# A mixture-of-experts stage rebuilt: plain scatters in place of adding ones, up weights fetched by address on VectorE

## What is computed

```python
h = tok(x)                                      # gather 36 angles per token, 6-qubit circuit, 192 features
h = h + attention(layernorm(h))                 # one head of 192, 512 x 512 scores per batch
z = layernorm(h)
scores = z @ Wg                                 # 8 experts
top2, which = top_k(scores, 2); share = softmax(top2)
h = h + sum_k share[k] * (gelu(z @ W1[which[k]] + b1[which[k]]) @ W2[which[k]] + b2[which[k]])
```

## Time and profile before

| What | us |
|---|---|
| median of 3 runs | 336.73 |
| lowest and highest of them | 336.37, 339.21 |
| span of the profiled execution | 338.6 |
| TensorE busy, matmuls | 240.9 |
| VectorE busy | 177.6 |
| ScalarE busy | 95.2 |
| POOL busy | 250.2 |

### The profile page before, as it was taken

One profiled execution on the slowest core, in us unless ns is written; L12 is line 12 of the kernel. 1 busy time (PEld: TensorE's weight loads), 2 busy tenths in 40 slices (PEclk: granted clock), 3 DMA queues, 4 the chain that ended last, 5 costly groups with the idle time before them and its releaser, 6 DMA issues. The chain is left out here.

```text
span 338.6 us, 6221 instructions
## 1 busy us (share of the span) xinstructions
PE 240.9 (71%) x1585; PEld 162.0 (48%) x1585; DVE 177.6 (52%) x698; ACT 95.2 (28%) x223; POOL 250.2 (74%) x283
## 2 busy tenths in 40 slices
PE   0831973668478989768654899999999587999500
PEld 0621641223243445444421678777777365877400
DVE  5758997488998866684699322232222122122200
ACT  1002001354324144634233323332432132133000
POOL 5778979309968777766777388888883888888673
PEclk9999995558955556965555599999999799699955
DMA  6710019900000001111123146656461556564510
GB/s 191 201 13 11 0 45 400 382 5 2 2 0 9 12 13 60 63 57 60 59 70 103 22 54 69 64 62 67 53 69 18 60 62 65 61 69 50 59 10 0
DMA packets 28141, 22.61 MB, mean 67 GB/s; under 512 B 15434, under 2 KB 25546, under 8 KB 27787
## 3 DMA queue, kind: packets, MB, share of 16 engines
q0 software_dynamic: 13296, 7.95, 21.1%
q1 hardware_dynamic: 14524, 14.23, 13.0%
q10 hardware_dynamic: 288, 0.03, 0.1%
HBM read 7.25 MB, written 15.63 MB: 68 GB/s over the span
## 5 line engine op out<-in xcount | busy, mean ns | idle before, releaser
L709 POOL DMA_INDIRECT out<-up x71 | 110.3, 1554 | 33.1 <-issue 13.9
L1972 PE MATMUL bank_b<-down,up 128*128 x426 | 91.2, 354 | 5.0 <-DVE up L1473 1.0
L1972 PEld LDWEIGHTS bank_b<-down,up 128*128 128x128 f32 x426 | 72.9, 200 | 22.6 <-issue 18.8
L1473 DVE TENSOR_SCALAR up<-bank_b,up 128x192 f32<-128x192 f32 x71 | 29.6, 418 | 97.5 <-PE bank_b L1972 84.9
L657 POOL DMA_INDIRECT routed<-rows,slot x64 | 61.9, 968 | 23.9 <-issue 18.0
L472 POOL DMA_INDIRECT theta_all<-angles,ids x32 | 32.4, 1012 | 10.9 <-issue 9.0
L1651 ACT ACTIVATE up<-bank_a 128x384 f32<-128x384 f32 x71 | 31.3, 497 | 3.4 <-PE bank_a L1962 2.9
L1775 PE MATMUL bank_b<-queries_t,keys_t 32*128 32x512 f32 x64 | 26.1, 900 | 6.9 <-ACT keys_t L1499 3.4
L1782 PE MATMUL bank_a<-keys_t,wt 32*128 32x512 f32 x64 | 27.6, 949 | 3.8 <-DVE nmax L1133 2.1
L1663 ACT COPY up<-bank_c 128x384 f32<-128x384 f32 x18 | 8.6, 478 | 61.8 <-PE bank_c L1951 58.7
L1133 DVE TENSOR_REDUCE nmax<-bank_a 128x2 f32<-128x1024 f32 x16 | 19.5, 1219 | 11.5 <-PE bank_a L1782 11.3
(11 more groups left out here) (420 smaller groups left out, 369.4 us busy)
## 6 DMA issues: line engine op xcount, KB each, us to landing
routed<-pad_rows SPq DMA_DIRECT2D x8, 528.0 KB, 5.7
out<-hres SPq DMA_DIRECT2D x8, 384.0 KB, 2.4
down<-down_w SPq DMA_DIRECT2D x1, 2304.0 KB, 11.9
up<-up_w SPq DMA_DIRECT2D x1, 1536.0 KB
out<-up POOLq DMA_INDIRECT x71, 3.5
up<-routed SPq DMA_DIRECT2D x69, 16.0 KB
routed<-rows,slot POOLq DMA_INDIRECT x64
up<-up_w SPq DMA_DIRECT2D x1, 780.0 KB
```

The costliest lines, as they stand in the source:

```text
L709: pool.indirect_dma_start(out=out_rows, out_offset=bass.IndirectOffsetOnAxis(xb[:, m // STEP % RING, m % STEP, DEST:DEST + 1].bitcast(I32) ...
L1473: dve.tensor_scalar(y[:, m % RESULTS, :], bank_b[:, m % 2, 0:D], xb[:, m // STEP % RING, m % STEP, SHARE:SHARE + 1], None, ALU.mult).then_ ...
L1972: mm = pe.matmul(bank_b[:, m % 2, 0:D], hid[:, m % STEP, c * P:(c + 1) * P], down[:, bass.ds(first + c * D, D)], start=(c == 0), stop=(c = ...
```

## The change

The experts' results are no longer added into `out`. They are scattered as plain rows into a tensor of their own, read back and added to `hres` on VectorE, and `out` is written once.

- **Scatters.** POOL's indirect DMA of a result writes to `shares_out`, 8192 rows of 192: row `k * 4096 + token` for choice k. `DEST` carries that number. No two blocks write one row, so the waits for blocks with common tokens, the table behind them and SyncE's counting go. POOL waits for the landing of block m - 4 (LAG) before it issues block m, and tells of it by `landed`.
- **Runs.** The blocks are put in another order: first the whole blocks that the first four batches fill, by expert, then those that each later batch completes, then the rest. The number of blocks stays 71. So results of early batches are complete before the last block. Of the blocks, 24 (EARLY) can be loaded before the second half's scatters have landed.
- **Table.** `block_table` holds a block's numbers in the partition of the block's own number, two per partition, so it works on 48 or so elements at a time where it had up to 568. Thirteen dependent stages follow its first.
- **Loads.** All 71 blocks have their own place in `xb` (no ring), and SyncE issues all loads, each behind its own value load.
- **Up weights.** TensorE merges each expert's up weights into 128 partitions, with the same 16 rows eight times over, and ScalarE copies them beside the down weights, into `wide` (eight copies). In the expert stage `pick_up`, `expert_of` and ScalarE's copy go. VectorE's `expert_up` reads the expert's address (`value_load`) and copies 32 partitions x 384 into `up_now`, four times a step.
- **Sums.** SyncE reads the two choices of a batch back (`load_sums`, 786 KB), VectorE adds them to `hres` (`add_experts`, four additions), and SyncE stores the batch. For batches 0 to 5 that stands between the weightings of blocks 51, 55, 59, 63, 65 and 67 and the next ones, for batches 6 and 7 behind the last.
- **Order.** TensorE's order in a step becomes down, up, down, down, transpose, down. ScalarE's gelus run three blocks further ahead of the copies of transposed blocks.

The diff, cut to its core:

```diff
+    LAG = 4
+    ADDS_AFTER = LAG + 2 * STEP
...
+    shares_out = nc.dram_tensor("shares_out", (2 * TOKENS, D), F32, kind="Internal").ap()
...
+            def load_block(m):
+                row = sp.value_load(t_i[m:m + 1, 0:1], min_val=0, max_val=ROWS - P)
+                sp.dma_start(xb[:, m, :], routed[bass.ds(row, P), :]).then_inc(block_in[m // STEP], 16)
+
+            def load_sums(b):
+                if b >= SUMS:
+                    sp.wait_ge(sum_done, b - SUMS + 1)
+                sp.dma_start(expert_sums[b % SUMS], shares_view[b]).then_inc(sums_in[b % SUMS], 16)
...
+            for b in range(BATCHES):
+                sp.wait_ge(landed, blocks_until(b))
+                load_sums(b)
+                if b > 0:
+                    store(b - 1)
+            store(BATCHES - 1)
...
-            pool.wait_ge(h2_out, 16 * BATCHES)
-            pool.wait_ge(order_done, 1)
             for m in range(BLOCKS):
-                last_shared = pool.value_load(t_i[0:1, 1, m:m + 1], min_val=1, max_val=BLOCKS + 1)
                 pool.wait_ge(y_done, m + 1)
-                pool.wait_ge(landed, last_shared)
-                hold(pool)
+                if m >= LAG:
+                    all_landed(m - LAG)
                 pool.indirect_dma_start(
...
+                    out=shares_out, out_offset=bass.IndirectOffsetOnAxis(xb[:, m, DEST:DEST + 1].bitcast(I32), 0),
+                    in_=y[:, m % RESULTS, :], in_offset=None, bounds_check=2 * TOKENS - 1,
+                    oob_is_err=False).then_inc(added[m % RESULTS], 16)
...
+            def add_experts(b):
+                dve.wait_ge(h2_copied, 2 * b + 2)
+                dve.wait_ge(sums_in[b % SUMS], 16 * (b // SUMS + 1))
+                half = TILES // 2 * D
+                for k in range(2):
+                    for x in (slice(0, half), slice(half, 2 * half)):
+                        total = dve.tensor_tensor(hres[:, b, x], hres[:, b, x], expert_sums[b % SUMS][:, k, x], ALU.add)
...
+            def expert_up(s):
+                if s >= 2:
+                    dve.wait_ge(hid_done, s - 1)
+                for n, m in enumerate(blocks_of(s)):
+                    r = slice(n * F, (n + 1) * F)
+                    first = dve.value_load(t_i[m:m + 1, 1:2], min_val=0, max_val=(E - 1) * WIDE)
+                    copied = dve.tensor_copy(up_now[r, s % 2, :], wide_flat[r, bass.ds(first + HC * D, HID)])
+                copied.then_inc(up_ready, 1)
...
             for m in range(BLOCKS):
                 weighted(m)
                 if m % STEP == 1 and m // STEP + 2 < STEPS:
-                    expert_of(m // STEP + 2)
+                    expert_up(m // STEP + 2)
+                elif m % 2 == 1 and m >= blocks_until(summed) + ADDS_AFTER:
+                    add_experts(summed)
+                    summed += 1
+            for b in range(summed, BATCHES):
+                add_experts(b)
...
-            up_copy()
+            for e in range(E):
+                up_copy(e)
...
-            pick_up(0)
-            pick_up(1)
...
             block_transpose(0)
             up_proj(0)
+            block_transpose(1)
             for m in range(BLOCKS):
                 s, n = divmod(m, STEP)
                 down_proj(m)
                 if n == 0 and s + 1 < STEPS:
-                    block_transpose(s + 1)
-                if n == 1 and s + 1 < STEPS:
                     up_proj(s + 1)
                 if n == 2 and s + 2 < STEPS:
-                    pick_up(s + 2)
+                    block_transpose(s + 2)
```

More of the change, by code:

```diff
@@ L350, in build @@
         landed = sem("landed")
+        up_ready = sem("up_ready")
+        sums_in = [sem(f"sums_in{n}") for n in range(SUMS)]
+        sum_done = sem("sum_done")
         passed = sem("passed")
@@ L354, in blocks_of, with blocks_until @@
             return range(s * STEP, min(s * STEP + STEP, BLOCKS))
+        def blocks_until(b):
+            for end in ENDS:
+                if b < end:
+                    return min(2 * end * SEQ // P + E - 1, BLOCKS)
         def part_of(b):
@@ L421, in rows_written @@
-            def rows_written(s):
-                least = sp.value_load(need[0:1, s:s + 1], min_val=16, max_val=16 + 16 * 2 * TILES * (BATCHES - SEEN))
-                sp.wait_ge(scattered_last, least)
-                hold(sp)
-            for b in range(BATCHES):
-                if b == 1:
-                    sp.wait_ge(scattered_last, 16)
-                    sp.sem_inc(first_marked, 1)
-                store(b)
-            sp.sem_inc(landed, 1)
-            sp.wait_ge(table_done, 1)
-            first_rows = [block_row(m) for m in range(0, STEP, 2)]
@@ L434, in _ @@
[L434 to L448 removed]
+            sp.wait_ge(table_done, 1)
@@ new lines, in _ @@
+            sp.wait_ge(scattered_early, 16 * 2 * TILES * HALF)
+            for m in range(EARLY):
+                load_block(m)
+            sp.wait_ge(scattered_late, 16 * 2 * TILES * (BATCHES - HALF))
+            for m in range(EARLY, BLOCKS):
+                load_block(m)
+            sp.wait_ge(exp_done, 2 * BATCHES)
+            sp.wait_ge(context_done, BATCHES)
+            for b in range(BATCHES):
+                sp.wait_ge(landed, blocks_until(b))
+                load_sums(b)
+                if b > 0:
+                    store(b - 1)
@@ L1971, in down_proj @@
                 for c in range(HC):
-                    mm = pe.matmul(bank_b[:, m % 2, 0:D], hid[:, m % STEP, c * P:(c + 1) * P], down[:, bass.ds(first + c * D, D)],
-                                   start=(c == 0), stop=(c == HC - 1))
+                    mm = pe.matmul(bank_b[:, m % 2, 0:D], hid[:, m % STEP, c * P:(c + 1) * P],
+                                   wide_flat[:, bass.ds(first + c * D, D)], start=(c == 0), stop=(c == HC - 1))
                 mm.then_inc(y_mm, 1)
```

323 lines of the change are left out of this document (125 added, 198 removed).

## The result

| | us |
|---|---|
| changed kernel, median of 4 runs (lowest, highest) | 350.39 (349.52, 353.41) |
| kernel before beside it, median of 4 runs | 337.12 |
| ratio, with its 95% interval | 1.0385 (1.0319 to 1.0451) |
| span and own time of the profiled execution | 347.8, 349.52 |
| VectorE busy, POOL busy | 202.3, 208.4 |

The account below looks back on a forecast made before the run. POOL's adding scatters were taken as the bound; VectorE's fetch would pace the new loop. Start 193.4, 16 steps of 7.3 us and last blocks gave 319.0, plus a 12.9 us tail 331.9: 330.0 us from the median, range 318 to 351.

Parts of the forecast that it names:

- The start: Expert stage's start: table in 3.4 us, ready at 178.6, 3.3 us earlier; first result weighted at 190.9, 2.2 us earlier.
- the first A of the loop: End of the first step's second down projection on TensorE, put at 193.4 us; the loop's sum starts there.
- The scatters: POOL's plain scatters with their gap: 1.35 us per block taken, between 1.26 and 1.86.
- POOL stays the pace: Rival: plain scatters keep 1.55 us, 71 x 1.86 = 132 us on POOL, 335 us in all; chance 0.07.
- The fetch: VectorE's four value loads (0.75 us each) and copies between two weightings: a 1.25 us TensorE hole, steps of 7.3 us.
- the rival of loads that wait: VectorE's value loads wait for running copies: fetch 4.4 us, step 8.7, 22 us more, 352 us; chance 0.10.
- the hidden fetch: Rival: VectorE's value loads cost half, the hole closes, TensorE paces at 5.9 to 6.4 us, 315 us; chance 0.14.
- the forecast without falls: Forecast as worked out, granted clock at 1.00 in the loop: 330.0 us, own range 325 to 335; chance 0.40.
- the one with falls: Rival: TensorE's hole lowers the granted clock in every second step, 8 x 1.4 = 11 us more, 341 us; chance 0.24.
- the last five blocks: Loop's end: no fetches, two batches of additions each holding TensorE about 1 us: 5 x 1.2 + 2.
- the tail: After the last weighting: last scatter, its landing, load of sums (3.9 us), additions (2.2), store (2.4): 12.9 us in all.
- collisions: Rival: VectorE's copies hold up POOL's descriptors; with scatters of 1.86 us, 8.8 us per step, 355 us; chance 0.05.

Follow-up runs that it names:

- The filled hole: Changed kernel plus two 128x384 matmuls nobody reads on TensorE behind each step's fourth down projection: 343.51 us, ratio 1.0106 to the kernel before.
- the run without copies: Changed kernel with VectorE's four value loads kept but the up-weight copies left out from the third step on: 329.23 us, ratio 0.972 to the kernel before.
- the run without value loads: Changed kernel with VectorE's copies kept, taking a fixed expert's up weights without any value load: 315.02 us in one run.

## Why the prediction was wrong

**The start came out right by luck.** The second weighting stood at 193.35, where I had put the first A of the loop (193.4), but by errors that cancel. The table took 3.7 us (I had 3.4), and it was ready at 175.76 and not at 178.6 because its first stage ran at 172.06, 3.2 us ahead of the one before. From the table to the first weighting it took 14.3 us, where I had 12.3. The second followed after 3.3 us, where I had 2.16; and my 193.4 adds a weighting's 0.4 to a distance that runs from start to start, so by my own terms it should have been 193.0.

**The scatters held.** 1.0 us where I took 1.05 with 0.30 of gap, and POOL was no longer the pace. The rival "POOL stays the pace" fell; row length cost next to nothing (975 ns for 32 numbers, 1007 for 192).

**The fetch was worked out right, up to a quarter of a us.** Loads every 0.75 us, the next weighting after 3.4 to 3.5 us, as written. The loads run beside copies, so the rival of loads that wait fell, and so did the hidden fetch. (The rival of loads that wait was priced too high: with 4.4 us of fetch in place of 3.4 it gives a step of 8.4, not 8.7, and some 348 us, not 352.) But TensorE was back earlier (its down projections take 1.17 us, not 1.2) and went on later: a hole of 1.7 to 2.4 us for most of the loop, not 1.25, and steps of 7.5, not 7.3. Two steps without a fall were longer still, 7.9 and 8.1 us. In the first of them the four copies ended 0.5 us later: the copy at 211.56, which started inside a scatter, took 0.61 us in place of 0.35, and a value load behind it 0.46 in place of 0.31.

**The step that failed is the clock, which the sum had at nothing.** "A hole of 1.25 us in every step may or may not be enough for that": I gave the forecast without falls 0.40 and the one with falls 0.24, with 17 us at 1.00 in the earlier trace rows as the argument against. That stretch had 3.6 us of idle time in it, but no hole of this length in each step, and so could not carry the argument. The filled hole shows the price, 7 us. In the run without copies a hole of 1.0 us in each step came with no fall in 100 us. In the rival I had counted eight falls in the sixteen steps and 341 us; five came, so even the rival with the right mechanism was too fast, for what follows.

**The second is the end of the loop.** I let the last five blocks take 5 x 1.2 + 2 = 8 us; from the weighting at 321.88 to 334.70 they took 12.8 (in the kernel with the filled hole, 12.7). A load of sums had been costed in the tail alone, at 3.9 us. Between blocks 65 and 67 the additions need one within the loop, and it took 7.8 us beside a store and the next load. Additions "cost nothing" only where their load has landed.

**The tail held**, 13.1 us against 12.9, with additions of 2.09 us (I had 2.2); the last load took about 4.8 us, not 3.9, but the last scatter had landed 2.2 us after its start, not 2.9.

The sum: 347.8 - 331.9 = 15.9 us of span, of which the loop's 16 steps are 321.88 - 311.0 = 10.9 (7 for the clock, 4 for the longer steps; the loop of the kernel with the filled hole, with no fall in it, was 6.3 us shorter), the last five blocks 4.8, the tail 0.2. The remaining 4.5 us to the median are the conversion: I took 1.9 off the span, but an execution's own time lies 1.7 above its span (349.52 and 347.8), and the runs' median a little higher.

Between the terms lies the reason for the wrong sign. The forecast of -2% was the difference of 7.3 and 7.4 us per step, plus gains at the start and the end: a pace as slow as the old one, with a new cause. Where two paces are that close, each thing the new one brings, a clock, a late load, can decide the sign, and all of them pointed one way. No single one did it: without the falls the ratio is 1.0106, where I had forecast 0.98. At least half of the chances should have lain on slower.

On collisions the Trainium skill (SBUF — State Buffer, section "SBUF: two separate sides") says that GpSimd and VectorE share a port pair, that whichever starts first holds it for its whole instruction, and that an fp32 copy from SBUF to SBUF is an operation that takes it. The rows of the changed kernel agree in size:

```profile
L696 POOL DMA_INDIRECT shares_out<-up x71: 982/985/1367, 191.3 to 335.6; - x71
...
L1430 DVE COPY up<-wide x71: 347/351/646, 176.8 to 317.5; 32x384 f32 x71
```

The longest scatter took 1367 - 985 = 0.38 us more than the median, about one copy's length, the longest copy 0.3 more, and the medians (985 and 351 ns) stand next to the shortest (982 and 347). Collisions had a part in a step or two that took 0.5 us longer and were not the reason for the result, as the run without value loads shows.

## What to carry to other kernels

An operation that moves to an engine with idle time is priced by what stands behind it in that engine's queue, not by the engine's busy share: split it into pieces and put one behind each result that another engine waits for. Count value loads as work of the sequencer (0.63 us each with their register operations here, 0.75 with a copy behind each), since the busy time does not hold them. And ask of every hole that a change opens in TensorE what it does to the granted clock; matmuls that nobody reads, put into the hole, are a cheap test of that.

## What the runs showed of the hardware that I had not expected

- The landing of a plain scatter took 2.3 us in the median and up to 7.4 us beside loads and stores of 384 to 768 KB, so a lag of four blocks was enough in most of the loop and not at its end (one wait of 2.27 us, at 319.2).
- A load of 768 KB took 4.7 to 6.2 us in the median by buffer, 7.8 at most, against the 4.4 of the line through the earlier trace rows.
- An indirect scatter's time on POOL went with adding (0.98 to 1.55 us) and hardly with the row's length (975 ns for 32 numbers, 1007 for 192).
